# Contracting 192 channels as 128 and 64 instead of 96 and 96, in the second block of a vision tower

## The chip, the cores and the metric

One core of a Trainium2 chip runs the whole kernel. The metric is the device time of one execution in microseconds (us). Before the change it is 1512.79 us, the median of 3 runs (1511.65 to 1516.04).

## The reference, cut to what matters

32 images become 49 tokens of 192 channels each: T = 1568 tokens. The tower has a first block (Mamba, then a soft mixture of 64 experts), which the change doesn't touch, and a second block:

```
h  = LN(x) ;  k = h Wk_a^T ; v = h Wv_a^T ; sr = sigmoid(h Wr_a^T)          (192 -> 192 each)
x  = x + (sr * bi_wkv(decay, first, k, v)) Wo_a^T
h  = LN(x) ;  kf = relu(h Wk_f^T)^2                                         (192 -> 768)
x  = x + sigmoid(h Wr_f^T) * (kf Wv_f^T)                                    (receptance, 768 -> 192)
h  = LN(x) ;  q, k, v = split(h in_w^T + in_b) ; 12 heads of 16, softmax over the 49 tokens of an image
x  = x + ctx out_w^T + out_b
x  = x + MLP(x) ;  x = x + mixture of 4 experts, 192 -> 768 -> 192 each
```

All of it is float32.

## The kernel before, in words

Every engine runs a program written by hand: the order on each engine is the order of the code, and semaphores carry the dependences. A `Stage` is a row of PSUM results: `fill` makes TensorE wait until the bank's last result was taken, `wait_filled` and `wait_taken` are the two sides, and `plan` gives each result its bank (eight of them) and the engine that takes it. A step below is one matrix multiplication of the program; in the profile it has two records, since its operands are float32.

Tokens stand in 16 tiles of 98 (two images), and in 4 quarters of 392 (NT = 16, QT = 392; half `h` is quarters 2h and 2h+1). What is contracted over channels must have channels on partitions, so each LayerNorm's output is turned by TensorE. In the parts that the change touches it is turned as two chunks of 96 channels (`transposed`, `turn`), and ScalarE copies it out of PSUM with LayerNorm's gain and bias (`turned_in` into `xaT`, `turned_x5` into `x5T` and, every image twice, into `x5two`). Each product is then two steps of 96 rows into one PSUM bank. The MLP and the experts at the end of the kernel already contract 128 and 64 rows (`packed`, `hidden_tiles`, `xmA`, `xmB`): four 128-row steps, then four 64-row steps that lie by turns on partitions 0 to 63 and 64 to 127.

The second block in order, by the functions of TensorE's program:

- `turn(s_xaT)`, `kvr_in(0)`, `kvr_in(1)`, `turn(s_xaT)`, then a loop over 6 units of `arguments`, `kvr_in(t + 2)` and `sums`. Units with `j == 0` make 128 of the 192 outputs for one quarter; units 2 and 3 make the last 64 outputs for two quarters, side by side in the array's columns. VectorE scans (`front`, `back`, `final`), ScalarE exponentiates.
- For each half: `turn(s_xbT)`, `receptance` (8 tiles, outputs of 98 x 192), `channel_hidden` (12 outputs of 128 x 392, taken by ScalarE with Relu and squared by VectorE), then `wkv_out(1)` in the first half only, and `channel_out`, which waits for `kf_ready`. `wkv_out` is the one function of this part that contracts 128 and then 64 rows already, by turns.
- `turn(s_x5T)` and `queries_keys` for each half (8 outputs of 96 x 392), with VectorE's `twice_normed` ahead of the turn. ScalarE takes them in `qk_out`; GpSimd spreads the keys into blocks (`kblk`, L907).
- The attention loop, one iteration for each of 16 pairs of images. TensorE: `value_rows(i)`, `score_rows(i)`, `prob_turn(i-1)`, `context_rows(i-2)`, `context_turn(i-3)`, `attention_out(i-4)`. VectorE: `values`, `less_max` (L1759, L1763), `context`, `sums`. ScalarE: `probs(i)` (Exp, L1298), `probs_t(i-1)`, `ctx_t(i-3)`. From iteration 4 on, the bank of `value_rows(i)` is the one that `ctx_t(i-4)` empties, and `ctx_t(i-4)` stands behind `probs(i-1)` on ScalarE.
- The bias of queries, keys and values is a 97th row: `in_w[CH]` holds it and `x5T`, `x5two` have a row of ones, which GpSimd writes (L894, L895).

L1876 is `mm`, L1885 the transposes of `transposed`, L923 ScalarE's `copy_out`, L1275 the doubled copy of `turned_x5`, L1386 `normalise`.

## Time and profile before

| | |
|---|---|
| median of 3 runs | 1512.79 us |
| the profiled execution, its own time | 1509.02 us |
| its span, first to last instruction | 1507.3 us |
| TensorE busy | 1323.9 us, 88% of the span |
| VectorE, ScalarE, GpSimd busy | 915.8, 670.9, 554.6 us |
| the second block up to the MLP | 895 to 1215 us of the span |

The profile is one execution. A busy TensorE says that a record was open, not that the array was full: ends of its records are modelled and overlap the next ones, so the pace is read from how many records start in a stretch. PE is TensorE, PEld its weight loads, DVE VectorE, ACT ScalarE, POOL GpSimd. PEclk is the granted share of TensorE's clock (1.00 is 2.4 GHz).

### The profile page before, as it was taken

What the parts mean: (1) busy time and instruction counts of PE and PEld (TensorE: products, weight loads), DVE (VectorE), ACT (ScalarE), POOL (GpSimd) and SP (SyncE); (2) the same over time, 40 slices, a digit from 0 to 9 for tenths busy, and PEclk for the clock granted to TensorE, in tenths of its full rate; (3) what the DMA queues carried; (4) which work ended last, traced back from release to release, by engine and by line L of the source; (5) the groups of instructions that cost most, each with busy time, mean ns of one, the idle gap of its engine ahead of it and who ended that gap; (6) DMA issues with size and microseconds to landing.
All of it is one profiled execution on the core that took longest, in us unless ns stands there. A gap on an engine that the chain in (4) does not pass through costs nothing.

```text
span 1507.3 us, 18440 instructions
## 1 busy us (share of the span) xinstructions
PE 1323.9 (88%) x6684; PEld 767.2 (51%) x6684; DVE 915.8 (61%) x1513; ACT 670.9 (45%) x1206; POOL 554.6 (37%) x399
## 2 busy tenths in 40 slices
PE   7979989898989867469988859979999999999998
PEld 6634445454545434244433445547856659445444
DVE  3789999999999999972100148855446624221022
ACT  4786767677777744042110117631552241313311
POOL 1478898988989887300000020012034302000000
PEclk9999999999999999769999969999999999999999
DMA  6405051422414040344999940000010001030101
GB/s 205 172 2 172 12 162 37 135 75 98 127 46 171 12 160 0 138 178 189 395 397 396 372 103 0 1 0 1 1 38 1 2 1 31 7 110 13 37 0 33
DMA packets 38773, 151.96 MB, mean 101 GB/s; under 512 B 10364, under 2 KB 14587, under 8 KB 33948
## 3 DMA queue, kind: packets, MB, share of 16 engines
q1 hardware_dynamic: 34588, 149.21, 27.6%
q10 hardware_dynamic: 4096, 1.58, 0.4%
q8 instruction: 54, 0.88, 0.2%
q14 instruction: 35, 0.29, 0.1%
HBM read 147.56 MB, written 1.63 MB: 99 GB/s over the span
## 4 chain that ended last, share of the span: by engine, by line
PE 54%; DVE 20%; issue 10%; ACT 6%; DMA 5%; POOL 4%; SPq 1%; ACTq 0%; DVEq 0%; POOLq 0%
PE ps L1876 52%; DVE arena L1474 7%; DVE arena L1463 5%; DMA arena<-in_e_b 4%; POOL arena L821 3%; ACT arena L923 2%; ACT ps L1034 1%; DVE stats L1371 1%; DVE arena L1759 1%; PE ps L1885 1%; ACT arena L928 1%; DVE arena L1483 1%; SPq L633 1%; DVE arena L1763 0%; DVE arena L1514 0%
## 5 line engine op out<-in xcount | busy, mean ns | idle before, releaser
L1876 PE MATMUL ps<-arena 128*32 128x192 f32 (+17 forms) x5236 | 946.4, 415 | 97.8 <-DVE arena L1524 22.2
L1876 PEld LDWEIGHTS ps<-arena 128*32 128x32 f32 (+15 forms) x5236 | 539.7, 154 | 475.7 <-issue 277.1
L821 POOL TENSOR_TENSOR arena<-arena 128x784 f32<-128x784 f32 x192 | 368.9, 1935 | 94.0 <-DVE arena L1474 93.4
L1876 PE MATMUL ps<-arena,ident 128*128 128x392 f32 x900 | 349.3, 517 | 48.3 <-POOL arena L821 40.0
L1474 DVE TENSOR_TENSOR_SCAN arena<-ps,arena 128x784 f32<-128x784 f32 x192 | 341.0, 1777 | 2.5 <-ACT ps L1034 2.5
L1876 PEld LDWEIGHTS ps<-arena,ident 128*128 128x128 f32 x900 | 169.6, 196 | 196.5 <-POOL arena L821 70.5
L1034 ACT ACTIVATE ps<-arena 128x384 f32<-128x384 f32 x384 | 207.9, 575 | 114.2 <-DVE arena L1474 113.4
L923 ACT ACTIVATE arena<-ps 128x392 f32<-128x392 f32 (+9 forms) x265 | 124.3, 487 | 294.7 <-PE ps L1876 206.2
L923 ACT ACTIVATE arena<-ps,arena 128x392 f32<-128x392 f32 (+2 forms) x191 | 103.4, 602 | 224.5 <-PE ps L1876 139.1
L1463 DVE TENSOR_TENSOR arena<-ps,arena 128x784 f32<-128x784 f32 x192 | 182.8, 953 | 8.0 <-ACT ps L1060 6.8
L1622 DVE COPY arena<-ps 128x384 f32<-128x384 f32 x32 | 16.3, 552 | 150.7 <-PE ps L2124 150.7
L1852 DVE SCALAR_TENSOR_TENSOR arena<-ps,arena 128x392 f32<-128x392 f32 x16 | 10.0, 626 | 127.3 <-PE ps L1876 112.0
L891 POOL TENSOR_TENSOR h<-h,arena 98x384 f32<-98x384 f32 x8 | 8.0, 996 | 152.5 <-DVE arena L1699 152.5
L907 POOL TENSOR_TENSOR arena<-arena 96x294 f32<-96x294 f32 x64 | 41.6, 681 | 56.8 <-PE ps L1876 53.5
L855 POOL MEMSET arena<- 128x128 f32 x1 | 0.2, 205 | 124.8 <-ACT arena L923 124.8
L873 POOL TENSOR_SCALAR arena<-arena 128x4 f32<-128x4 f32 x1 | 0.2, 236 | 122.7 <-DMA arena<-in_first 122.7
L1885 PE MATMUL ps<-ident,arena 98*96 98x98 f32 x160 | 21.9, 283 | 23.5 <-ACT arena L1146 17.3
L1298 ACT ACTIVATE arena<-arena 113x588 f32<-113x588 f32 x16 | 11.1, 694 | 62.5 <-DVE arena L1763 62.5
L1785 DVE TENSOR_TENSOR arena<-arena,ps 98x192 f32<-98x192 f32 x32 | 11.1, 354 | 45.6 <-PE ps L1876 44.0
L914 POOL TENSOR_TENSOR h<-h,arena 98x192 f32<-98x192 f32 x16 | 9.3, 593 | 71.7 <-DVE arena L1785 71.7
L1885 PEld LDWEIGHTS ps<-ident,arena 98*96 98x96 f32 x160 | 17.4, 145 | 30.6 <-ACT arena L1146 18.8
L923 ACT ACT_TABLE_LOAD x10 | 12.8, 1283 | 45.2 <-PE ps L1876 45.1
(201 smaller groups left out, 861.0 us busy)
## 6 DMA issues: line engine op xcount, KB each, us to landing
arena<-in_e_w SPq DMA_DIRECT2D x32, 2304.0 KB
arena<-bc_rows SPq DMA_DIRECT2D x128, 392.0 KB, 4.8
arena<-in_patches SPq DMA_DIRECT2D x4, 1176.0 KB, 7.5
arena<-comb_rows SPq DMA_DIRECT2D x1, 3136.0 KB, 10.7
arena<-in_mlp_w SPq DMA_DIRECT2D x5, 576.0 KB, 4.6
arena<-arena ACTq DMA_DIRECT2D x128, 12.0 KB, 8.6
arena<-in_mlp_w SPq DMA_DIRECT2D x5, 384.0 KB, 3.6
arena<-in_mlp_w SPq DMA_DIRECT2D x10, 192.0 KB, 4.0
```

The source lines that it names most:

```text
L633: sp.dma_start(dst, src).then_inc(loaded[key], 16)
L821: pool.tensor_tensor(pair(hbuf[:, at % SLOTS, :]), pair(hbuf[:, at % SLOTS, :]), c_all[:, n:n + 2, :], ALU.mult).then_inc(times_c, 1)
L907: pool.tensor_tensor(kblk[:, 4 * (i % 2) + 2 * j + c, :].rearrange("p (h l) -> p h l", l=TOKENS), kT[:, c, at:at + TOKENS].unsqueeze(1).br ...
L923: act.activation(dst, src, func, **kw).then_inc(s.taken["act"], 1)
L928: ins = act.activation(dst[r][:, k, :], ident[:, :], ACT.Copy, scale=values(k))
L1034: ins = act.activation(steps_of(two(DECAY[at % 2], 128, HALF)[:, j * QT:(j + 1) * QT])[:, :, lo:lo + TOKENS - 1], steps_of(dt[:, s % 2, c, ...
L1371: own.step(dve.bn_stats(stats[:, t, :], src[:, i, :]))
L1463: TT(pair(hbuf[:, at % SLOTS, :]), bank(DU_BANK, 128, 0, QT).unsqueeze(1).broadcast_to([128, 2, QT]), b_all[:, 2 * p:2 * p + 2, :], ALU.mu ...
L1474: dve.tensor_tensor_scan(hbuf[:, at % SLOTS, :][:, way], dA[:, way], hbuf[:, at % SLOTS, :][:, way], 0.0, ALU.mult, ALU.add).then_inc(scan ...
L1622: dve.tensor_copy(hidT[:, g % 2, 3 * k:3 * k + 3, :].rearrange("p k n -> p (k n)"), bank(s_hT.banks[i][0], 128, 0, 384)).then_inc(s_hT.tak ...
L1876: return pe.matmul(dst, lhsT, rhs, start=first, stop=last)
L1885: ins = pe.transpose(bank(s.banks[i][0], parts, t * TILE, (t + 1) * TILE), src[:, 4 * q + t, chunk(c)], ident[0:TILE, 0:TILE])
```

## The change

Channel mix, receptance, and attention's queries, keys and values contract 128 and 64 rows. The turned activations become a wide tensor (128 rows, all tokens) and a narrow one (channels 128 to 191 of quarters 2h on partitions 0 to 63, of quarters 2h+1 on 64 to 127); each narrow weight stands twice, on both halves of the partitions. `packed` turns each half as wide, wide, narrow, narrow, so a product waits for a later item of the turn. The 97th rows are gone: `qk_out` adds the bias of queries and keys, and `ctx_t`, now two activations instead of one, that of the values. GpSimd's two memsets go, one load less is issued in group `tb`, and the channel-mix products come out by hidden chunk instead of by quarter, so `channel_out` waits for nearly all squares.

```diff
-        xaT = R.take(CH, [2, T])
+        xaA = R.take(128, [T])
+        xaB = R.take(128, [HALF])
...
-                        s_xaT.wait_taken(pe, 2 * q + 1)
-                        for c in range(2):
-                            ins = mm(bank(s_kvr.banks[i][0], 128, 0, QT), w_kvr[:, c, w * D:w * D + 128],
-                                     xaT[:, c, quarter(q)], c == 0, c == 1)
+                        h, k = divmod(q, 2)
+                        s_xaT.wait_taken(pe, 4 * h + 2 + k)
+                        dst, rows = bank(s_kvr.banks[i][0], 128, 0, QT), slice(64 * k, 64 * k + 64)
+                        mm(dst, w_kvr[:, 0, w * D:w * D + 128], xaA[:, quarter(q)], True, False)
+                        ins = mm(dst, w_kvr[rows, 1, w * D:w * D + 128], xaB[rows, h * QT:(h + 1) * QT], False, True)
...
             def receptance(k):
 
+                s_xbT.wait_taken(pe, 4 * k + 3)
+                for first in range(4 * k, 4 * k + 4, 2):
+                    both = [(n, 2 * pair_at(n) + j) for j in range(2) for n in (first, first + 1)]
+                    for n in (first, first + 1):
+                        s_rf.fill(pe, n)
+                    for n, tile in both:
+                        dst = bank(s_rf.banks[n][0], TILE, tile % 2 * D, (tile % 2 + 1) * D)
+                        p0 = 64 * (tile // TQ % 2)
+                        at = tile // 8 * QT + tile % TQ * TILE
+                        mm(dst, xaA[:, cols(tile)], w_rf[:, 0, :], True, False)
+                        ins = mm(dst, xaB[p0:p0 + 64, at:at + TILE], w_rf[p0:p0 + 64, 1, :], False, True)
+                        if tile % 2 == 1:
+                            ins.then_inc(s_rf.filled, 1)
+
+            def channel_hidden(k):
+
+                for first in range(12 * k, 12 * k + 12, 4):
+                    for i in range(first, first + 4):
+                        _, m, j = WIDE[i]
+                        s_kf.fill(pe, i)
+                        mm(bank(s_kf.banks[i][0], 128, 0, QT), w_kf[:, 0, 128 * m:128 * m + 128],
+                           xaA[:, quarter(2 * k + j)], True, False)
+                    for i in range(first, first + 4):
+                        _, m, j = WIDE[i]
+                        rows = slice(64 * j, 64 * j + 64)
+                        mm(bank(s_kf.banks[i][0], 128, 0, QT), w_kf[rows, 1, 128 * m:128 * m + 128],
+                           xaB[rows, k * QT:(k + 1) * QT], False, True).then_inc(s_kf.filled, 1)
...
-                    pe.wait_ge(kf_ready, 6 * (i // 2) + 6)
+                    pe.wait_ge(kf_ready, 12 * k + 11 + i // 2 % 2)
...
             def value_rows(i):
                 s_vb.fill(pe, i)
                 for j in range(2):
-                    at = (2 * i + j) * TILE
-                    for k in range(2):
-                        rows = CH + k
-                        ins = mm(bank(s_vb.banks[i][0], TILE, j * D, (j + 1) * D),
-                                 x5two[0:rows, k, at:at + TILE],
-                                 in_w[0:rows, k, 2 * D:3 * D], k == 0, k == 1)
+                    image = 2 * i + j
+                    p0 = 64 * (image // 8 % 2)
+                    at = (image // 16 * 8 + image % 8) * TILE
+                    dst = bank(s_vb.banks[i][0], TILE, j * D, (j + 1) * D)
+                    mm(dst, x5twoA[:, image * TILE:(image + 1) * TILE], in_w[:, 0, 2 * D:3 * D], True, False)
+                    ins = mm(dst, x5twoB[p0:p0 + 64, at:at + TILE], in_w[p0:p0 + 64, 1, 2 * D:3 * D], False, True)
...
             def ctx_t(i):
                 v = bank(s_cx.banks[i][0], CH, 0, 2 * 128).rearrange("p (c j q) -> p c j q", c=2, j=2)
-                copy_out(s_cx, i, ctxT[0:CH, :, cols(i)].rearrange("p c (j l) -> p c j l", j=2),
-                         v[:, :, :, 0:TOKENS])
+                s_cx.wait_filled(act, i)
+                for c in range(2):
+                    ins = act.activation(ctxT[0:CH, c, cols(i)].rearrange("p (j l) -> p j l", j=2),
+                                         v[:, c, :, 0:TOKENS], ACT.Identity, bias=in_b[:, 4 + c:5 + c])
+                ins.then_inc(s_cx.taken["act"], 1)
```

`kvr_in`'s units 2 and 3 become, for each of k, v and r, two wide steps side by side and then two narrow ones side by side. `queries_keys` is written like `channel_hidden`: four wide steps, then four narrow ones, two groups to a half; `queries_keys` waits for the fourth item of the turn. `turned_x5` still makes two activations for each of its 8 items.

The order on TensorE from the first half's receptance to the first half's `channel_out` (ps2 and ps3 hold the receptance, then `channel_hidden` runs through the banks). Before:

```order
L1885 MATMUL ps0<-ident,arena 96x98 x8
L1885 MATMUL ps1<-ident,arena 96x98 x8
L1876 MATMUL ps2<-arena 98x192 x8
L1876 MATMUL ps3<-arena 98x192 x8
L1876 MATMUL ps0<-arena 128x392 x4
L1876 MATMUL ps1<-arena 128x392 x4
L1876 MATMUL ps2<-arena 128x392 x4
L1876 MATMUL ps3<-arena 128x392 x4
```

And in the changed kernel, at the same place:

```order
L2193 MATMUL ps0<-ident,arena 128x98 x8
L2193 MATMUL ps1<-ident,arena 128x98 x8
L1897 MATMUL ps2<-arena 98x192 x8
L1897 MATMUL ps3<-arena 98x192 x8
L1897 MATMUL ps0<-arena 128x392 x2
L1897 MATMUL ps1<-arena 128x392 x2
L1897 MATMUL ps0<-arena 128x392 x2
L1897 MATMUL ps1<-arena 128x392 x2
```

The number of steps is the same everywhere. In `channel_hidden` four banks are opened by wide steps and then closed by narrow ones; in the receptance the rows read alike, and inside them wide and narrow steps now take turns.

The order on ScalarE in the attention loop, one iteration (Exp, the copy of the turned probabilities, the turned context). Before:

```order
L1298 ACTIVATE arena<-arena 113x588
L923 ACTIVATE arena<-ps3 98x678
L923 ACTIVATE arena<-ps0 96x2x98
```

In the changed kernel:

```order
L1316 ACTIVATE arena<-arena 113x588
L937 ACTIVATE arena<-ps3 98x678
L1330 ACTIVATE arena<-ps0,arena 96x98 x2
```

The turned context is taken by two activations with a bias where one copy stood.

## Rows read from the trace of the kernel before

**Rows 1.** The page: busy time of each engine, and the chain that ended last.
```profile
PE 1323.9 (88%) x6684; PEld 767.2 (51%) x6684; DVE 915.8 (61%) x1513; ACT 670.9 (45%) x1206; POOL 554.6 (37%) x399
PE 54%; DVE 20%; issue 10%; ACT 6%; DMA 5%; POOL 4%; SPq 1%; ACTq 0%; DVEq 0%; POOLq 0%
```

**Rows 2.** The chain that ended last, second block: start us, us, what.
```profile
898.62 9.66 PE ps L1876 x24
...
940.51 54.15 PE ps L1876 x172
...
1009.81 44.78 PE ps L1876 x208
```

**Rows 3.** Windows: stretch, length, PE, PEld, DVE, ACT, POOL busy (xcount), PEclk, DMA.
```profile
1009.82:1015.09 5.27, 5.27 (x32) 5.27 (x33) 0.00 (x0) 2.55 (x5) 0.00 (x0) 1.00 0.02 3
1015.10:1030.89 15.79, 15.79 (x49) 9.09 (x49) 6.24 (x11) 5.96 (x12) 0.00 (x0) 1.00 0.00 0
1030.90:1038.74 7.84, 7.84 (x33) 3.85 (x31) 2.23 (x4) 0.50 (x1) 2.99 (x3) 1.00 0.01 2
1295.34:1301.33 5.99, 5.99 (x16) 0.70 (x16) 1.84 (x3) 0.00 (x0) 0.00 (x0) 1.00 0.00 0
1363.71:1368.04 4.33, 4.33 (x18) 2.11 (x16) 0.00 (x0) 1.94 (x6) 0.00 (x0) 1.00 0.00 0
```

**Rows 4.** Timeline of the turns: start us, us, engine line, [idle before <-releaser].
```profile
895.48 3.14 PE L1885 MATMUL ps<-ident,arena 98*96 98x98 f32 x16 [4.09 <-DVE arena L1386]
896.78 2.55 ACT L923 ACTIVATE arena<-ps,arena 96x392 f32<-96x392 f32 x4 [23.17 <-PE ps L1885]
...
1008.52 2.38 ACT L923 ACTIVATE arena<-ps,arena 96x392 f32<-96x392 f32 x4 [7.98 <-PE ps L1885]
```

**Rows 5.** Timeline of the turn ahead of queries and keys, second half.
```profile
1100.18 0.18 DVE L1361 SCALAR_TENSOR_TENSOR rs<-rs_tmp,rs 98x16 f32<-98x16 f32 x1
1100.34 5.21 POOL L907 TENSOR_TENSOR arena<-arena 96x294 f32<-96x294 f32 x8 [3.25 <-ACT arena L923]
1100.39 0.67 DVE L1359 SCALAR_TENSOR_TENSOR rs_tmp<-var,rs 98x16 f32<-98x16 f32 x1
1103.00 3.82 DVE L1386 TENSOR_SCALAR arena<-h,mv,rs 98x192 f32<-98x192 f32 x8
...
1107.52 1.00 ACT L1275 ACTIVATE arena<-ps,arena 96x784 f32<-96x784 f32 x1
1108.41 0.67 ACT L923 ACTIVATE arena<-ps,arena 96x392 f32<-96x392 f32 x1
```

**Rows 6.** Windows again: second half's queries and keys; the attention loop's 16 starts.
```profile
1109.13:1121.37 12.24, 12.24 (x32) 5.93 (x33) 0.00 (x0) 9.38 (x19) 0.00 (x0) 0.86 0.00 1
1121.38:1207.80 86.42, 79.78 (x757) 55.57 (x755) 55.72 (x120) 23.60 (x45) 36.41 (x56) 1.00 0.01 1
```

**Rows 7.** Timeline of one iteration of the attention loop, and the next one's start.
```profile
1172.04 2.69 PE L1876 MATMUL ps<-arena 96*98 96x192 f32 x16 [0.41 <-ACT arena L923]
1173.52 0.69 PEld L1876 LDWEIGHTS ps<-arena 96*64 96x64 f32 x8 [0.25 <-issue]
...
1175.58 0.83 DVE L1763 TENSOR_TENSOR arena<-ps,arena 113x294 f32<-113x294 f32 x2
1176.45 0.69 ACT L1298 ACTIVATE arena<-arena 113x588 f32<-113x588 f32 x1 [4.46 <-DVE arena L1763]
1177.05 0.93 ACT L923 ACTIVATE arena<-ps 98x678 f32<-98x678 f32 x2
1178.04 2.68 PE L1876 MATMUL ps<-arena 96*98 96x192 f32 x16 [0.41 <-ACT arena L923]
```

**Rows 8.** Groups by line and shape, 880 to 1300 us: xcount, busy us, mean ns.
```profile
L923 ACT ACTIVATE arena<-ps 128x392 f32<-128x392 f32 x64 | 31.7, 497 | 42.2 <-PE ps L1876 40.2 <-PE ps L2393 2.0
L923 ACT ACTIVATE arena<-ps,arena 128x392 f32<-128x392 f32 x58 | 31.1, 594 | 55.6 <-PE ps L2393 30.5 <-PE ps L1876 25.0
...
L923 ACT ACTIVATE arena<-ps 96x196 f32<-96x196 f32 x16 | 5.1, 321 | 3.1 <-PE ps L2359 3.1
```

More of the change, by code:

```diff
@@ L316, in build_tower @@
         mlp2b = R.take(TILE, [D])
-        aff5 = R.take(CH, [2, 2])
+        aff5 = R.take(128, [2, 2])
+        in_b = R.take(CH, [6])
         aff_m = R.take(128, [2, 2])
@@ L1199, in turned_in @@
                 for i in some:
-                    q, c = divmod(i, 2)
-                    copy_out(s, i, xaT[:, c, quarter(q)], bank(s.banks[i][0], CH, 0, QT),
-                             ACT.Identity, bias=aff[:, row + 1, c:c + 1], scale=aff[:, row, c:c + 1])
+                    rows, c = rows_of(i)
+                    copy_out(s, i, turned(i, xaA, xaB), turning(s, i),
+                             ACT.Identity, bias=aff[rows, row + 1, c:c + 1], scale=aff[rows, row, c:c + 1])
             def kvr_out(u):
@@ L2160, in _, with packed @@
                 ins.then_inc(s_mix.filled, 1)
+            def packed(s, src, ready, some=range(8)):
+                flat = src.rearrange("p t n -> p (t n)")
+                for i in some:
+                    h, c, k = i // 4, i // 2 % 2, i % 2
+                    s.fill(pe, i)
+                    for t in range(TQ):
+                        at = 8 * h + TQ * k + t
+                        ready(at + 1 if c == 1 and k == 0 else at)
+                        lo = at * D + (0 if c == 0 else 128 if k == 0 else 64)
+                        ins = pe.transpose(bank(s.banks[i][0], 128, t * TILE, (t + 1) * TILE),
+                                           flat[:, lo:lo + 128], ident[0:TILE, 0:TILE])
+                    ins.then_inc(s.filled, 1)
             def kvr_in(u):
@@ L2261, in turn @@
             def turn(s, src, ready, k):
-                transposed(s, src, lambda i: pe.wait_ge(ready, i + 1), some=range(4 * k, 4 * k + 4))
+                packed(s, src, lambda i: pe.wait_ge(ready, i + 1), range(4 * k, 4 * k + 4))
             pe.wait_ge(loaded["rw"], 16 * RW_LOADS)
@@ L2291, in _ @@
             pe.wait_ge(loaded["tb"], 16 * TB_LOADS)
-            pe.wait_ge(const_ready, MIX_CONST + 2)
+            pe.wait_ge(const_ready, MIX_CONST + 1)
             def queries_keys(some):
-                for i in some:
-                    q, which, c = i // 4, i // 2 % 2, i % 2
-                    s_x5T.wait_taken(pe, 2 * q + 1)
-                    s_qk.fill(pe, i)
-                    for k in range(2):
-                        rows = CH + k
-                        at = which * D + c * CH
-                        ins = mm(bank(s_qk.banks[i][0], CH, 0, QT), in_w[0:rows, k, at:at + CH],
-                                 x5T[0:rows, k, quarter(q)], k == 0, k == 1)
-                    ins.then_inc(s_qk.filled, 1)
+                for first in range(some.start, some.stop, 4):
+                    h = first // 8
+                    s_x5T.wait_taken(pe, 4 * h + 3)
+                    for i in range(first, first + 4):
+                        at, q = i % 8 // 2 * CH, 2 * h + i % 2
+                        s_qk.fill(pe, i)
+                        mm(bank(s_qk.banks[i][0], CH, 0, QT), in_w[:, 0, at:at + CH], x5A[:, quarter(q)], True, False)
+                    for i in range(first, first + 4):
+                        at, rows = i % 8 // 2 * CH, slice(64 * (i % 2), 64 * (i % 2) + 64)
+                        mm(bank(s_qk.banks[i][0], CH, 0, QT), in_w[rows, 1, at:at + CH],
+                           x5B[rows, h * QT:(h + 1) * QT], False, True).then_inc(s_qk.filled, 1)
             queries_keys(range(8))
```

140 lines of the change are left out of this document (63 added, 77 removed).

## The prediction

> **What bounds the kernel now.** First the page: TensorE is busy for 88% of the span and carries 54% of the chain that ended last [rows 1]. An average over stages says little about five functions, so next the chain itself in the second block: it runs on TensorE alone for 9.66 us of `kvr_in`, for 54.15 us in the loop that holds the other units of `kvr_in`, and for 44.78 us from receptance to `channel_out` [rows 2]. There a step saved or lengthened counts in full. Two places are different. Between `channel_out(1)` and the second half's queries, VectorE's LayerNorm and ScalarE's eight copies bound the time [rows 5]. In the attention loop TensorE waits in every iteration, for ScalarE: the idle time ahead of `value_rows` is ended by ACT L923 [rows 7].
>
> **What a change between 128 and 64 rows costs.** The diff keeps the number of steps. It can gain only where narrow steps stand next to each other on opposite halves, and it loses wherever wide and narrow steps meet. Both are in the trace, in functions written that way already. The first 32 records of `receptance(0)`, all of 96 rows, take 5.27 us, so a step of two records takes 0.33 us [rows 3]. `wkv_out(1)` has as many steps of the same shape, but 128 and 64 rows by turns: 7.84 us, 0.98 us for a pair instead of 0.66 [rows 3]. That is 0.33 us for two changes, 0.165 each. With outputs of 392 columns a step takes 15.79 / 24 = 0.658 us [rows 3]. The experts' group of four wide and four narrow ones takes 4.33 us (4.35 with the windows' edges) [rows 3]; four wide and two double narrow ones would be 6 x 0.658 = 3.95, so two changes cost 0.40. The gate's four pairs, with weights of 4 columns only, take 5.99 us, 1.50 a pair against 1.32: 0.18 for two changes [rows 3]. So a change costs 0.09 us with next to no weights to load, and 0.17 to 0.20 with 98 to 128 columns of them.
>
> The Trainium skill speaks to this on its page "TensorEngine Tiling (Array Packing)", in two places. Tiling Modes, Key Properties: changing the tiling mode, not just the tile, drains the array. By that rule this change pays at each border, and the trace agrees. The page's section on theoretical speedup gives up to 2x for contractions of 64 rows or fewer, which speaks for the change; no function of this trace reaches it over wide and narrow steps together (the experts' group gets 5.26 / 4.35 = 1.21 times).
>
> **The change part by part.**
>
> 1. Turn ahead of `kvr_in(0)`. It waited for item 2 of the turn, now for item 3. ScalarE takes the four in 2.55 us from 896.78, so the third is done at about 898.9, and TensorE starts now at 898.4 [rows 4]. +0.6 us.
> 2. `kvr_in`, four units of one quarter: 12 pairs wide, narrow, never two narrow ones together. Each pair has two changes of 128 columns: 12 x 0.39 = +4.6. Bounds: the gate's 0.18 gives 2.2, the experts' 0.40 gives 4.8; I take the latter's side, since the weights have 128 columns.
> 3. `kvr_in`, two units of 64 outputs: side by side in columns before and after, with two narrow steps between wide ones. Changes go from 2 to 7 a unit. Weights of 64 columns lie between 4 and 98, so 0.14 each: +1.4. The trace doesn't show this change of rows under divided columns: 0 to 2.0.
> 4. Turns ahead of receptance, twice. TensorE waited for two of four items, now for all. ScalarE takes four in 2.38 us from 1008.52, to 1010.90, and receptance started at 1009.81 [rows 2, 4]: +1.1 each, +2.3.
> 5. Receptance, twice 8 pairs. The second tile's narrow step is on the other half, but a wide step stands between, so I price it like `wkv_out`, whose shape it has: 7.84 - 5.27 = 2.6 each, **+5.2**.
> 6. `channel_hidden`, twice: 3 groups of 4.35 instead of 15.79: -2.75 each, **-5.5**. ScalarE and VectorE now take four results in a burst, and `channel_out(1)` waits for nearly all squares instead of half; only a turn lies between: +0.2.
> 7. Queries and keys. The first half's 16 steps lie under VectorE's LayerNorm, so what they save there is worth nothing in itself. The turn behind it now has to be copied out whole: 4 x 1.46 us on ScalarE (an L1275 and an L923, 1107.52 to about 1108.97) instead of 2 x 1.46 [rows 5]. But the keys' blocks on GpSimd start later, since the first key item is now in the second group. Today, when GpSimd starts at 1100.34, VectorE's next small step takes 0.67 us where it took 0.18 just before, and eight `normalise` take 3.82 [rows 5]. Without that the tiles are there some 3 us earlier, and ScalarE starts at about 1104.9, behind the first half's copies, instead of 1106.05. It ends at about 1110.7 instead of letting TensorE go at 1109.13: +1.6. Then 4.35 x 2 = 8.7 us instead of 10.5: -1.8. The stretch of 12.24 us has a granted clock of 0.86 after the idle time [rows 6], and TensorE is idle for longer now: +0.3. Together +0.1, between -2 if nothing else is late and +3 if GpSimd collides as before.
> 8. `value_rows`, 16 iterations. Now 1.48 us from 1172.04 to the scores' first weights at 1173.52 [rows 7], already with a change at the end. Afterwards two of `wkv_out`'s pairs, 1.96 to 1.98: **+0.5** each. What hides it? Nothing: the ring is values and scores on TensorE, maximum and subtraction on VectorE to 1176.41, Exp at 1176.45, two copies from 1177.05 to 1177.98, and `value_rows` at 1178.04, since it waits for the bank that `ctx_t` empties [rows 7]. 16 x 0.5 = **+8.0**. VectorE and GpSimd move with the ring.
> 9. `ctx_t` as two activations with a bias. A copy of 392 columns takes 0.497, of 196 columns 0.321 us, so 0.9 ns a column and 0.23 us for 98; a bias adds 0.594 - 0.497 = 0.10 [rows 8]. Two of 0.33 that overlap by 0.10, like their neighbours, are 0.55 instead of 0.32: +0.22, on the ring for `value_rows(4)` to `value_rows(15)`, 12 x 0.22 = +2.6, and 0.4 in the tail. Bounds 0.15 and 0.35 give 1.8 and 4.6.
> 10. At nothing: the two memsets on GpSimd (they ran under `channel_out(0)`; nothing waited), wider loads of weights (VectorE holds TensorE until 895.48, not a load [rows 4]), transposes of 128 instead of 96 columns, and the bias in `qk_out`, 16 times 0.1 us on an engine that is idle between items; were that cover gone, it would be 0.8 us in the second half.
>
> Sum: 0.6 + 4.6 + 1.4 + 2.3 + 5.2 - 5.5 + 0.2 + 0.1 + 8.0 + 3.0 = **+19.9 us**. The profiled execution took 1509.0 us, so it would take 1529. The median of the runs shown is 3.8 us above it; the forecast for the median is 1512.8 + 19.9, about 1533.
>
> **The rivals.**
>
> - *No border costs anything here, and narrow steps on opposite halves overlap even with a wide one between (faster, 0.04).* This is the tiling page's up to 2x, as a mechanism of this kernel: receptance saves 8 of 32 steps, 8 x 0.33 = -2.6, `channel_hidden` saves 12 x 0.658 = -7.9, the queries' section -0.7, `kvr_in` and `value_rows` nothing; against it 0.6 + 2.3 + 3.0 for the later waits and `ctx_t`, with 0.2 for the squares. -5.1: 1507.7. For it speaks only that receptance goes from half to half on purpose. Against it, `wkv_out`'s 7.84 us. It decides if a wide and narrow pair of receptance takes under 0.6 us, not 0.98.
> - *The borders are free, but nothing overlaps across a wide step (same, 0.03).* Then only item 5 is zero instead of -2.6: -2.5, 1510.
> - *The attention loop absorbs its part (slower by less, 0.12).* TensorE has 0.41 us idle ahead of `value_rows` [rows 7]. If the ring is another than I read, items 8 and 9 are hidden: +8.9, 1522. Against it, TensorE restarts 0.05 us after ScalarE's end in every iteration.
> - *The clock falls as well (slower by more, 0.10).* With more waiting in the loop (79.78 us busy of 86.42 now [rows 6]) the granted clock may not stay at 1.00, as it doesn't behind the idle time of [rows 6]. A tenth of the loop at half clock would be some 8 us: 1541.
> - *The forecast (0.71)*: 1533.
>
> **How the numbers follow.** Bounds of the unknown costs: item 2 -2.4, item 3 -1.4 to +0.6, item 7 -2 to +3, item 9 -1 to +2, and 2 to 3 us between medians. Rarely all one way: 1527 to 1539 for the forecast alone. The range reaches down to the loop that absorbs and up to the clock: 1521 to 1542. A measurement of this kernel can tell about 0.3%, 4.5 us, from no change. Slower: 0.71 + 0.12 + 0.10 = 0.93; same 0.03; faster 0.04.
>
> **What would show it.** In the new profile: an iteration of the attention loop of about 6.7 us instead of 6.0, with 1.98 us from the first value step to the scores; receptance of 7.8 us; `channel_hidden` of 13 us a half; `kvr_in`'s pairs at 1.7 us; VectorE's small steps ahead of the last turn at 0.18 us throughout. The forecast is wrong if receptance's 32 records take about 5 us, or if iterations stay at 6.0 us.

## The result, and the profile after

The changed kernel takes 1562.59 us in the median (1555.98 to 1584.12, 4 runs), beside 1513.40 for the kernel before (1511.65 to 1516.04, 4 runs): a ratio of 1.0309, interval 1.0249 to 1.0369. Every ratio here and below leaves out executions over 1.5% above the fastest of their kernel (one of the four here, three of ten for `ctx_t` as two activations alone, two of four for receptance grouped). The profiled execution took 1555.98 us against 1509.02, +47.0. The forecast was 1533 and its range ended at 1542. The four executions of the changed kernel differ by 28 us among themselves, and the longer ones have the lower mean granted clock (0.934 at 1555.98 us, 0.912 at 1584.12). Only the first was profiled; a trace of a later execution of the same kernel, below, differs from it in the attention loop.

First the page: busy time, the granted clock over the 40 slices, and the chain's shares. They answer to [rows 1]. TensorE is busy for 35 us more with the same 6684 records, and its share of the chain is still over half.

```profile
PE 1359.1 (87%) x6684; PEld 761.8 (49%) x6684; DVE 910.7 (59%) x1513; ACT 675.2 (43%) x1222; POOL 548.9 (35%) x397
...
PEclk9989999999999999689999769969999979989999
...
PE 52%; DVE 19%; issue 10%; ACT 7%; POOL 5%; DMA 5%; SPq 1%; ACTq 0%; DVEq 0%; POOLq 0%
```

Next the chain that ended last in the second block (start us, us, what), which answers to [rows 2]. `kvr_in(0)` and `kvr_in(1)` are 19.28 us where they were 9.66, receptance to `channel_out` 50.89 where it was 44.78.

```profile
896.13 19.28 PE ps L1897 x24
...
1026.02 50.89 PE ps L1897 x208
...
1079.85 21.05 PE ps L1897 x80
```

The windows of the changed kernel say what the steps cost at either clock (columns as in [rows 3]). TensorE is idle for 4.09 us ahead of the turn (first line, timeline), as in the kernel before [rows 4]; then the turn and the 24 records of `kvr_in` run at a granted clock of 0.50 (1.2 GHz) from end to end, 3.20 us a pair. Two pairs of `kvr_in` at 1.00 (2.4 GHz) take 3.41 us, a unit of 64 outputs takes 4.84. Receptance of the second half takes 7.80 at 1.00; what stands at the same place in the first half, 36 records, takes 15.39 at 0.56.

```profile
892.26 3.66 PE L2193 MATMUL ps<-ident,arena 98*128 98x98 f32 x16 [4.09 <-DVE arena L1407]
```

```profile
896.13:915.34 19.21, 19.21 (x24) 5.97 (x24) 15.11 (x50) 3.05 (x6) 0.00 (x0) 0.50 0.00 1
...
1026.02:1041.41 15.39, 15.39 (x36) 7.32 (x37) 0.00 (x0) 1.96 (x4) 0.00 (x0) 0.56 0.00 0
1079.80:1087.60 7.80, 7.75 (x32) 3.94 (x32) 5.77 (x32) 1.47 (x3) 0.00 (x0) 1.00 0.01 2
...
956.83:960.24 3.41, 3.41 (x9) 1.18 (x8) 3.38 (x5) 0.99 (x2) 0.00 (x0) 1.00 0.01 2
926.67:931.51 4.84, 4.84 (x25) 1.18 (x24) 4.81 (x9) 1.58 (x3) 0.00 (x0) 1.00 0.00 0
```

One iteration of the attention loop, from the timeline, answers to [rows 7]. From the first value step at 1201.25 to the scores' weights at 1203.23 are 1.98 us, where they were 1.48. `ctx_t` is two activations in 0.56 us, and TensorE's idle time ahead of `value_rows` is 0.65 us, ended by them. From Exp to Exp it is 6.75 us.

```profile
1199.42 0.69 ACT L1316 ACTIVATE arena<-arena 113x588 f32<-113x588 f32 x1 [4.97 <-DVE arena L1784]
...
1200.64 0.56 ACT L1330 ACTIVATE arena<-ps,arena 96x98 f32<-96x98 f32 x2
...
1201.25 3.19 PE L1897 MATMUL ps<-arena 128*98 128x192 f32 x16 [0.65 <-ACT arena L1330]
...
1203.23 0.69 PEld L1897 LDWEIGHTS ps<-arena 96*64 96x64 f32 x8 [0.25 <-issue]
...
1206.17 0.69 ACT L1316 ACTIVATE arena<-arena 113x588 f32<-113x588 f32 x1 [4.97 <-DVE arena L1784]
```

**Where the 47 us lie.** Seven stretches, each between marks that both traces have (the first transpose of a turn, the first and the last Exp; for receptance's first turn the first step of the last `sums`, which stands right ahead of it, 4 us before its first transpose):

| stretch | before, us | after, us | more | forecast |
|---|---|---|---|---|
| start to the second block's first turn | 895.5 | 892.3 | -3.2 | 0 |
| to receptance's first turn (`kvr_in` lies here) | 108.6 | 126.1 | +17.5 | +6.6 |
| to receptance's second turn | 50.3 | 58.4 | +8.1 | +1.0 |
| to the turn ahead of `channel_out(1)` | 22.9 | 24.0 | +1.1 | +1.0 |
| to the first Exp (queries and keys) | 48.5 | 48.3 | -0.2 | +0.3 |
| first to last Exp | 80.7 | 92.6 | +12.0 | +10.1 |
| last Exp to the end | 300.9 | 312.6 | +11.7 | +0.9 |

Where the clock is 1.00 the forecast fits. The rest stands where the granted clock is 0.50. Read in windows of 1 us, it is at 0.50 behind 891 us for 30.7 us (6.8 in the kernel before), at 1014 and 1028 us for 23.9 (6.8, at 1001), at 1130 for 6.8 (3.4, at 1110), from 1236 to 1260 for 23.9 (none), and behind 1320 for 13.6 (3.4). The stretch from 1236 begins in the loop and covers its end:

```profile
1241.69:1260.00 18.31, 18.24 (x127) 15.11 (x124) 5.71 (x16) 6.78 (x16) 0.00 (x0) 0.50 0.00 1
```

### The profile page after: what moved, and what is told of

Same layout as the page of the kernel before. It is cut to its first block, busy times and chain, and to the rows that moved or that the text cites. A ratio compares the mean times of both kernels' runs of the same rounds, so it can differ in the third digit from the quotient of the medians.

```text
span 1554.3 us, 18438 instructions
## 1 busy us (share of the span) xinstructions
PE 1359.1 (87%) x6684; PEld 761.8 (49%) x6684; DVE 910.7 (59%) x1513; ACT 675.2 (43%) x1222; POOL 548.9 (35%) x397
## 4 chain that ended last, share of the span: by engine, by line
PE 52%; DVE 19%; issue 10%; ACT 7%; POOL 5%; DMA 5%; SPq 1%; ACTq 0%; DVEq 0%; POOLq 0%
PE ps L1897 50%; DVE arena L1495 7%; DVE arena L1484 5%; DMA arena<-in_e_b 4%; POOL arena L837 4%; ACT arena L937 2%; PE ps L2193 1%; ACT ps L1048 1%; DVE arena L1535 1%; DVE arena L1780 1%; ACT arena L942 1%; DVE stats L1392 1%; DVE arena L1504 1%; SPq L650 1%; POOL arena L848 0%
## 5 line engine op out<-in xcount | busy, mean ns | idle before, releaser
L1897 PE MATMUL ps<-arena 128*32 128x192 f32 (+17 forms) x5236 | 974.8, 421 | 107.4 <-ACT arena L937 24.4
L1897 PEld LDWEIGHTS ps<-arena 128*32 128x32 f32 (+16 forms) x5236 | 528.9, 156 | 522.9 <-issue 330.9
L937 ACT ACTIVATE arena<-ps 128x392 f32<-128x392 f32 (+9 forms) x233 | 111.1, 498 | 298.7 <-PE ps L1897 199.3
L937 ACT ACTIVATE arena<-ps,arena 128x392 f32<-128x392 f32 (+2 forms) x207 | 112.2, 601 | 246.5 <-PE ps L1897 159.9
L1806 DVE TENSOR_TENSOR arena<-arena,ps 98x192 f32<-98x192 f32 x32 | 11.1, 354 | 49.6 <-PE ps L1897 48.3
L1768 DVE TENSOR_TENSOR arena<-ps,arena 98x384 f32<-98x384 f32 x16 | 8.9, 558 | 47.1 <-PE ps L1897 47.1
L1731 DVE TENSOR_TENSOR arena<-arena 128x392 f32<-128x392 f32 x24 | 12.0, 562 | 36.5 <-ACT arena L937 36.5
```

Source lines behind the costliest of these rows:

```text
L937: act.activation(dst, src, func, **kw).then_inc(s.taken["act"], 1)
L1897: return pe.matmul(dst, lhsT, rhs, start=first, stop=last)
```

## The experiments

Two theories on why the clock is low for so long. A border is a place where a 128-row step and a 64-row step meet. **A:** places thick with borders between 128-row and 64-row steps hold it down. **B:** TensorE waits longer (for whole turns, for `ctx_t`), and that lets it fall. In all figures below the ratio is to the kernel before on the same chip.

**The changed kernel again.**

> The changed kernel as it is, once more, to see how far its executions differ. From 890 us on the profile of the changed kernel had a granted clock of half speed for 99 us, where the kernel before had it for 20 us. Theory A (the borders between 128-row and 64-row steps hold the clock down, wherever they are dense): 1555 to 1570 us, half clock again in kvr_in and receptance. Theory B (the longer waits of TensorE let the clock fall, and where it falls is a matter of phase): the same mean, but the stretches at half clock move about between executions.

1574.26 us (1571.18 to 1578.39, 4 runs), 1.0389 [1.0357, 1.0421]. The stretches up to the loop repeat within 2 us (125.1 for 126.1, 59.9 for 58.4). The loop doesn't: it runs at 0.50 from 1197 us to its end and beyond, 85.3 us in one go. Windows of the loop:

```profile
1150.53:1196.90 46.37, 42.25 (x374) 25.03 (x372) 28.11 (x60) 13.95 (x29) 21.80 (x34) 1.00 0.00 1
1196.95:1264.07 67.12, 67.12 (x342) 39.89 (x343) 24.79 (x52) 11.30 (x24) 12.97 (x20) 0.50 0.00 1
```

An iteration is 6.74 us at 1.00 and 10.23 at 0.50: 3.5 us lost in each. The median is over the 1570 expected at most: the loss in the loop varies more than one trace told.

**The waits alone.** The kernel before, waiting for later items of the turns:

```diff
-                        s_xaT.wait_taken(pe, 2 * q + 1)
+                        s_xaT.wait_taken(pe, 3 if q < 2 else 7)
-                    s_xbT.wait_taken(pe, 2 * (i // 2) + 1)
+                    s_xbT.wait_taken(pe, 4 * k + 3)
-                    s_x5T.wait_taken(pe, 2 * q + 1)
+                    s_x5T.wait_taken(pe, 4 * (q // 2) + 3)
```

> The kernel before, without any border more, but with the changed kernel's waits on the turns: kvr_in, receptance and queries_keys wait for the last item of their half instead of the second. Structure alone: 0.6 + 2.3 + 3 = 6 us more. Theory A: the clock stays as it was, 1518 to 1521 us, half speed for 20 to 30 us from 890 us on. Theory B: the clock falls as in the changed kernel, 1535 us or more with 60 us or more at half speed.

1519.71 us (1517.09 to 1526.22, 10 runs), 1.0037 [1.0019, 1.0056]. The stretch of `kvr_in` is 111.4 us, 2.8 more than before, and at 0.50 for 10.2 us behind 895. Theory A's number. The waits at the turns cost what they are long and take the clock down by little: from 890 to 1300 us its trace is at 0.50 for 30.6 us, that of the kernel before for 17.0, that of the changed kernel for 85.2.

**`value_rows` without borders.** The changed kernel, its narrow step on all 128 rows, with zero weights in the other half:

```diff
-                    ins = mm(dst, x5twoB[p0:p0 + 64, at:at + TILE], in_w[p0:p0 + 64, 1, 2 * D:3 * D], False, True)
+                    ins = mm(dst, x5twoB[:, at:at + TILE], in_w2 if p0 else in_w[:, 1, 2 * D:3 * D], False, True)
```

> The changed kernel with one thing other: value_rows contracts its 64 channels over all 128 rows, with weights that are zero on the other half's 64 rows, so it has no border between 128-row and 64-row steps and the same number of steps. The ring's own price goes back by 0.5 us an iteration (6.74 to about 6.24 us), 8 us in all. Theory A (borders hold the clock down): no stretch at half clock in the attention loop in any profile, so a median of 1540 to 1548 us beside some 1574 for the changed kernel. Theory B (longer waits do it; the loop's second activation for ctx_t stays): the 8 us alone, 1562 to 1567 us, half clock still in the loop.

1546.06 us (1543.99 to 1550.96, 4 runs), 1.0233 [1.0204, 1.0262]. An iteration is 6.23 us instead of 6.74: the borders of `value_rows` cost 0.51 us, forecast 0.5. The time is what theory A gave. TensorE still waits 0.65 us ahead of `value_rows`, and yet the clock is 1.00 all over the loop in the trace; that it was so in all four executions is taken from their narrow spread. The edit takes away the borders and puts more rows to work at once, so it doesn't tell these two apart:

```profile
1156.41:1239.65 83.24, 74.27 (x728) 51.84 (x724) 52.35 (x113) 24.62 (x53) 34.86 (x54) 1.00 0.01 1
```

**`ctx_t` as two activations, alone.** The kernel before with that part (bias zero):

```diff
-                copy_out(s_cx, i, ctxT[0:CH, :, cols(i)].rearrange("p c (j l) -> p c j l", j=2),
-                         v[:, :, :, 0:TOKENS])
+                s_cx.wait_filled(act, i)
+                for c in range(2):
+                    ins = act.activation(ctxT[0:CH, c, cols(i)].rearrange("p (j l) -> p j l", j=2),
+                                         v[:, c, :, 0:TOKENS], ACT.Identity, bias=act_c[0:CH, 5:6])
+                ins.then_inc(s_cx.taken["act"], 1)
```

> The kernel before, with ctx_t as two activations with a bias (of zeros), as in the changed kernel, and nothing else. An iteration of the attention loop goes from 6.00 to 6.24 us, so 3 to 4 us more in both theories. Theory A: 1517 to 1518 us and no half clock in the loop. Theory B: the longer wait of TensorE brings half clock into the loop, 1525 us or more.

An iteration of 6.24 us, +0.24 (forecast +0.22), and 1512.8 us of span in the profiled execution. But the ten executions go from 1508.21 to 1546.61, median 1524.14, where thirteen of the kernel before stay within 1507.58 to 1520.05. The ratio is 1.0038 [1.0003, 1.0074]. The three longest (1539 to 1547 us) have a mean granted clock of 0.926 to 0.932, the others 0.944 to 0.958. The profiled one is among the short ones, at 1.00 all over the loop, so where the clock was lost in the long ones isn't shown. No step of TensorE was changed, so theory A alone doesn't fit the loop.

**Receptance grouped by height.** The changed kernel, each two tiles' steps as wide, narrow, narrow, wide:

```diff
-                        mm(dst, xaA[:, cols(tile)], w_rf[:, 0, :], True, False)
-                        ins = mm(dst, xaB[p0:p0 + 64, at:at + TILE], w_rf[p0:p0 + 64, 1, :], False, True)
+                    order = [(0, both[0:2]), (1, both[0:2]), (1, both[2:4]), (0, both[2:4])]
...
+                                ins = mm(dst, xaA[:, cols(tile)], w_rf[:, 0, :], step < 2, step >= 2)
...
+                                ins = mm(dst, xaB[p0:p0 + 64, at:at + TILE], w_rf[p0:p0 + 64, 1, :],
+                                         step >= 2, step < 2)
```

> The changed kernel with receptance in groups: two wide steps, four narrow ones that lie by turns on either half, two wide ones, so 2 borders for 4 tiles in place of 8. A half's receptance goes from 7.84 to about 4.6 us at full clock, 6.5 us less in both theories. Theory A: the half clock behind the turn of the first half (1026 to 1043 us) is shorter as well, another 3 to 5 us there. Theory B: it stays for 14 to 17 us.

1566.01 us (1533.56 to 1580.27, 4 runs), 1.0212 [1.0128, 1.0296]: the total says little, since the executions differ by 47 us. The profiled execution has a loop at 1.00 and a span of 1531.8. Its two stretches of receptance are 48.80 and 20.69 us instead of 58.39 and 24.03, both under the kernel before (50.3, 22.9). In the second half, at 1.00 on either side, that is 3.3 us (3.25 expected). In the first it is 9.6, so some 6 us come from the clock, more than theory A's 3 to 5; the half clock at 1028 us is gone:

```profile
1016.70:1065.50 48.80, 47.65 (x230) 33.79 (x231) 19.64 (x60) 9.31 (x20) 3.98 (x4) 0.94 0.00 1
1065.51:1086.20 20.69, 19.11 (x98) 11.27 (x95) 12.57 (x48) 8.08 (x18) 0.00 (x0) 1.00 0.00 1
```

**`kvr_in` on 128 rows throughout** (the other half's weights zero, so no borders; it also waits for the last item of the turn):

```diff
-                        ins = mm(dst, w_kvr[rows, 1, w * D:w * D + 128], xaB[rows, h * QT:(h + 1) * QT], False, True)
+                        ins = mm(dst, low[:, w * D:w * D + 128], xaB[:, h * QT:(h + 1) * QT], False, True)
```

> The changed kernel with kvr_in's 64 channels contracted over all 128 rows with zeros in the weights: no border in kvr_in. Own price of its borders: 6 us less (24 changes of 0.2 and 14 of 0.14). Theory A: the stretch at half clock from 893 to 921 us shrinks to the 7 to 10 us that the kernels without borders have, another 9 us: 15 us less in all. Theory B: 6 us less, the stretch stays as long in time as TensorE has waited ahead of it.

1559.76 us (1556.72 to 1567.35, 4 runs), 1.0327 [1.029, 1.0363]. The stretch of `kvr_in` falls from 126.1 to 110.9 us, the half clock behind 891 us from 30.7 to 10.2. The total hardly moves, because the loop was at 0.50 for 65 us in the profiled execution.

**`kvr_in` grouped.** Is it the borders, or the 64-row steps? The same steps and rows as the change, in another order, and into three PSUM banks instead of two by turns:

```diff
-                        mm(dst, w_kvr[:, 0, w * D:w * D + 128], xaA[:, quarter(q)], True, False)
-                        ins = mm(dst, w_kvr[rows, 1, w * D:w * D + 128], xaB[rows, h * QT:(h + 1) * QT], False, True)
+                for w in range(3):
...
+                        mm(bank(s_kvr.banks[i][0], 128, 0, QT), w_kvr[:, 0, w * D:w * D + 128],
+                           xaA[:, quarter(q)], True, False)
...
+                for w in range(3):
...
+                        ins = mm(bank(s_kvr.banks[i][0], 128, 0, QT), w_kvr[rows, 1, w * D:w * D + 128],
+                                 xaB[rows, h * QT:(h + 1) * QT], False, True)
```

> The changed kernel, with each unit of kvr_in written as three wide steps and then three narrow ones, into three banks: 2 changes of height a unit instead of 6, the same steps and rows. From the first turn of the second block to the first turn ahead of receptance the changed kernel takes 126.1 us, the one before 108.6, and the changed one with 128 rows in every step of kvr_in 110.9. If borders are what costs and what holds the granted clock down (theory A), this stretch falls to 112 to 117 us and the half clock behind 891 us lasts 10 us instead of 31. If it is the 64-row steps themselves, fewer rows at work, that hold the clock down, only 16 borders of 0.2 go, and the stretch is 121 to 124 us. The whole time scatters with the attention loop, 1540 to 1575.

1558.30 us (1556.44 to 1562.59, 4 runs), 1.0302 [1.0279, 1.0325]. The stretch is 110.45 us; 6.8 us of it at 0.50 behind 892. `kvr_in(0)` and `kvr_in(1)` take 9.63 us instead of 19.28. It is the borders: the rows at work are the same, and the third bank isn't it, since the run on 128 rows kept two banks and took 110.9. 15.6 us come back, where the borders saved are worth some 5 us at 1.00 (four units with 4 changes less each and two with 5 less, 26 of 0.2 us or less). The second window is the loop, again at half clock:

```profile
893.75:1004.20 110.45, 102.17 (x346) 54.67 (x347) 91.27 (x202) 64.42 (x109) 3.98 (x4) 0.96 0.00 1
...
1196.30:1261.10 64.80, 64.73 (x357) 42.54 (x357) 22.78 (x52) 14.14 (x32) 7.80 (x12) 0.50 0.00 1
```

All sixteen traces of this case agree on `kvr_in` and the first receptance. `kvr_in` by turns (five traces) is at 0.50 for 27.3 to 30.7 us; grouped (five), for 6.8; without borders (six), for 6.8 to 10.2. Every trace has 6.8 to 10.2 us at 0.50 around the turn ahead of the first receptance; in the receptance behind it, steps by turns (six traces) have another 13.6 to 17.1, steps grouped or on 96 rows (ten) none or 3.4.

`value_rows` with its own steps grouped (two wide, then two narrow) was planned, alone and with the other two groupings, and has no measured time. So in the loop the borders were only ever taken away by padding to 128 rows.

**A longer ring without a border.** The kernel before, with `ctx_t` as four activations:

```diff
+                for c in range(2):
+                    for j in range(2):
+                        at = i * TILE + j * TOKENS
+                        ins = act.activation(ctxT[0:CH, c, at:at + TOKENS], v[:, c, j, 0:TOKENS],
+                                             ACT.Identity, bias=act_c[0:CH, 5:6])
```

> The kernel before, with ctx_t cut into four activations instead of one copy: the attention loop's ring is made longer on ScalarE alone, no step of TensorE is changed, and the output is the same. Two activations made an iteration 6.24 us instead of 6.00; four should make it about 6.6 to 6.7, as long as the changed kernel's 6.74. If longer waits of TensorE in the loop are what lets the granted clock fall there (theory B for the loop), some iterations take some 10 us at half clock in most executions, the executions scatter, and the median lies between 1530 and 1565. If borders between 128-row and 64-row steps are what does it (theory A for the loop), the granted clock stays at 1.00 over the loop, and the time is 1514 + 12 x 0.65 + 1, about 1523, with little scatter.

1544.55 us (1535.67 to 1546.67, 4 runs), 1.0188 [1.0157, 1.0219]: theory B's range, for the loop of this kernel. An iteration is 6.53 us, a little less than the 6.6 expected. TensorE is idle for 0.94 us ahead of `value_rows` (timeline), 0.41 before. The granted clock is 1.00 for the first nine iterations, and from 1173.7 us it is 0.50 (windows), with 9.49 us an iteration. The other three executions weren't traced; their times and mean granted clocks (0.927 to 0.935, beside 0.947 to 0.955 for the kernel before) say the same of them:

```profile
1166.23 0.85 ACT L1315 ACTIVATE arena<-ps,act_c 96x49 f32<-96x49 f32 x4
...
1167.13 2.68 PE L1882 MATMUL ps<-arena 96*98 96x192 f32 x16 [0.94 <-ACT arena L1315]
```

```profile
1124.20:1173.70 49.50, 42.77 (x421) 29.82 (x417) 31.74 (x68) 17.79 (x47) 24.43 (x38) 1.00 0.01 1
1173.74:1227.87 54.13, 54.13 (x293) 37.62 (x295) 21.04 (x44) 10.89 (x30) 10.38 (x16) 0.50 0.00 1
```

**Neither in the loop.** The changed kernel with `value_rows` on 128 rows, as above, and `ctx_t` as one copy, as in the kernel before.

> The changed kernel, with value_rows contracting 128 rows twice (the second time half of them zero weights, so no border) and ctx_t as one copy again; the bias of the values is left out of the computation. An iteration should be 6.00 us, as before the change. Theory B for the loop: no wait is longer than before, so the loop's granted clock is 1.00 in every execution, and the time is that of the kernel with value_rows at 128 rows, 1546, less 12 x 0.24 and 0.4: about 1543, all executions within 8 us. Theory A says the same of the loop, since no border is left in it; both leave the clock's loss in kvr_in and in receptance where it is. If the time is under 1530, the loss in those two stages hung on the loop's state after all, and both are wrong.

1543.04 us (1538.96 to 1549.03, 4 runs), 1.0197 [1.0168, 1.0225], where 1543 was expected. An iteration is 5.99 us at 1.00. `kvr_in` and the first receptance lose as in the changed kernel. That the median hits 1543 is partly luck: the executions differ by 10 us, and in the traced one (1546.94) the second receptance is at 0.50 for 17.1 us too, where no other trace has over 3.4.

**Borders in the loop, no longer wait.** The changed kernel with `kvr_in` and receptance grouped and `ctx_t` as one copy, `value_rows` as in the change. Against it, **the longer wait on 128 rows**: grouped, `value_rows` on 128 rows, `ctx_t` as four activations.

> The changed kernel with kvr_in and receptance grouped by height and ctx_t as one copy (the values' bias is left out of the computation), value_rows with its borders as in the change. An iteration is 6.00 + 0.50 = 6.50 us, as long as in the run with four activations and no border, but made longer by borders in the array and not by a wait. If a longer ring alone lets the clock fall, the two go alike: 1530 to 1550 for both, or 1516 for both. If borders count by themselves, only this one falls; if the drained array counts as work, only the other one does. With the clock at 1.00 over the loop it is 1511.1 + 16 x 0.5 = about 1519.

> The run with three edits (value_rows on 128 rows, no border, an iteration of 6.23 us, 1511.3, twelve executions without a fall in the loop) with ctx_t cut into four activations, as in the run that lengthened the ring of the kernel before: an iteration of about 6.53 us. There, with value_rows on 96 rows, the clock fell in the loop in all four executions (1536 to 1547). If the length of TensorE's wait decides, it falls here too: some iterations of 9.5 us, a median of 1530 to 1550. If it is what the steps have in height (rows 96 against 128), it does not, and the time is 1511.3 + 12 x 0.3 + 1 = about 1516, within 8 us of it.

The first: 1518.23 us (1517.06 to 1522.94, 10 runs), 1.0033 [1.0017, 1.0049]. Iterations of 6.50 us, made longer by borders, TensorE's idle time 0.41 us as before the change: the clock stays at 1.00 over the loop (first row). The second: 1522.26 us (1516.92 to 1526.62, 10 runs), 1.0058 [1.0037, 1.008]. Iterations of 6.53 us, idle time 0.94: two short falls in the loop, 3.4 us each, mean 0.96 (second row). Its time lies between what the two readings gave. With the same 0.94 us the 96-row kernel lost the clock for 72 us in one go.

```profile
1122.03:1210.23 88.20, 81.90 (x730) 48.72 (x728) 52.42 (x113) 21.75 (x41) 34.79 (x54) 1.00 0.01 1
```

```profile
1125.93:1215.65 89.72, 77.51 (x728) 53.93 (x724) 52.33 (x113) 28.18 (x77) 34.80 (x54) 0.96 0.01 1
```

All traces, by TensorE's idle time ahead of `value_rows` and by its steps; time at 0.50 that begins in the loop:

| steps of `value_rows` | 0.41 us | 0.65 us | 0.94 us |
|---|---|---|---|
| 96 rows | none (3 traces) | none (1; three of ten executions long) | 71.7 us (1) |
| 128 rows, padded | none (2) | none (2) | twice 3.4 us (1) |
| 128 and 64 by turns | none (1) | none (1), 23.9 to 85.3 us (4) | not run |

Neither theory stands alone. The borders of `value_rows` without a longer wait lose nothing, and a wait of 0.65 us without them lost nothing on 128 rows; the changed kernel has both, and taking away either one (the padding, or the single copy) takes the fall away. A wait of 0.94 us brings falls with no border, short or long by the steps.

**The account closed.** All four edits: `kvr_in` grouped, receptance grouped, `value_rows` on 128 rows, `ctx_t` as one copy; then the same with the change's two activations and bias, so that nothing is left out.

> The changed kernel with four edits at once: kvr_in's steps grouped by height, receptance's steps grouped by height, value_rows on 128 rows twice, ctx_t as one copy (the bias of the values is left out of the computation). It closes the account. The kernel with the last two took 1543.0; grouping kvr_in took 15.6 us off its stretch (126.1 to 110.5), grouping receptance 9.6 and 3.4 off the two stretches of the receptance (58.4 to 48.8, 24.1 to 20.7). If the lost time is made of these pieces alone, each in its own place, the sum is 1543.0 - 28.6 = 1514.4, between 1509 and 1519, with the half clock behind 891 us and behind 1010 us as short as in the kernel before, and an iteration of 6.00 us. If taking the clock's loss away in one place only moves it to another, as grouping kvr_in alone seemed to do with the attention loop, it is above 1525.

> As the run with four edits, but with ctx_t as two activations with the values' bias, as in the changed kernel, so that nothing is left out. An iteration is 6.24 us. With the clock at 1.00 over the loop it would be 1514.4 + 3.3 = about 1518. The kernel before with the same two activations had the loop's clock fall in some of its ten executions (1508 to 1547). If the lengthened ring alone brings that, this one scatters as well, 1515 to 1550, with a median of 1518 to 1535; if not, all executions are within 8 us of 1518. Either way it stays above the kernel before with the channel mix alone changed, 1510.5.

1511.11 us (1509.45 to 1515.70, 10 runs), 0.999 [0.9974, 1.0006], and 1511.30 us (1509.75 to 1519.15, 12 runs), 0.9995 [0.9977, 1.0012]. The loss is made up of these pieces, each in its own place (1514.4 expected, 1509 to 1519). The second, at 6.23 us an iteration and 0.65 us of idle time, shows no fall in the loop in its trace and no execution over 1519.15; its median is 7 us under the 1518 expected.

**What of the change pays.** The kernel before, with the channel mix's second part alone: its turn as 128 and 64 rows, receptance grouped, `channel_hidden` in fours. `kvr_in`, queries and keys, `value_rows` and `ctx_t` stay.

```diff
-            turn(s_xbT, xa, xb_ready, 0)
+            turn_xb(0)
             receptance(0)
             channel_hidden(0)
```

> The kernel before, with the part of the change that should pay alone: the second turn of each half as 128 and 64 rows, receptance with steps in groups of like height (wide, narrow, narrow, wide; two tiles' narrow ones on opposite halves), channel_hidden in fours as in the changed kernel. kvr_in, queries_keys, value_rows and ctx_t stay as they were. With receptance so grouped the changed kernel took 69.5 us from the turn ahead of receptance to the turn ahead of the second half's end, where the kernel before takes 73.2; so this one should be 3.5 us under it: ratio 0.9977, 1510 to 1512. If the longer waits ahead of receptance let the clock fall instead (theory B for that stage), the ratio is 1.000 to 1.003.

1510.48 us (1506.99 to 1516.37, 12 runs), beside 1514.63 (16 runs): 0.9975 [0.996, 0.9989]. It has the lowest ratio of all, and the only interval under 1, but the gain is 0.25%. In its trace the two stretches of receptance and `channel_hidden` take 48.70 and 22.39 us, 71.1 beside 73.2: 2.1 of the 4.2 us. Where the rest comes from isn't shown.

## Why the prediction was wrong

The direction was right, and so was the sum where the clock is at 1.00, nearly term by term. What failed is what the forecast put outside the sum: it priced every border at full clock.

- *A border.* 0.33 to 0.40 us for two. Two pairs of `kvr_in` take 3.41 us at 1.00, 1.71 a pair (forecast 1.7); the same 26 records around a unit of 64 outputs take 5.67 instead of 4.92 us (below): +0.75, for two units 1.5 (forecast 1.4). Receptance 7.80 (7.84). Items 2, 3 and 5 stand at 1.00. (In item 2, 12 x 0.39 is 4.7, not 4.6; nothing hangs on it.)

```profile
927.00 4.92 PE L1876 MATMUL ps<-arena 128*128 128x392 f32 x26
...
925.92 5.67 PE L1897 MATMUL ps<-arena 128*128 128x392 f32 x26
```

- *Waits at the turns.* From the first transpose of the turn to `kvr_in(0)` it is 3.9 us instead of 2.9, +0.9 (item 1: +0.6); to the second receptance 3.1 instead of 1.8, +1.3 (item 4: +1.1). The run with the waits alone, which has one more of them (ahead of queries and keys), took 5.5 us more in the median where 6 were expected.
- *`channel_hidden`.* The second half's stretch is +1.1 us as summed, 7.80 us of receptance and 21.05 for it and the hidden part together, so 13.25 (item 6: 3 x 4.35 = 13.05).
- *Queries and keys.* -0.2 us for +0.3. GpSimd's blocks no longer meet VectorE's small steps, which take 0.17 us throughout (timeline of the changed kernel, in place of the 0.67 us of [rows 5]).

```profile
1124.57 0.17 DVE L1382 SCALAR_TENSOR_TENSOR rs<-rs_tmp,rs 98x16 f32<-98x16 f32 x1
...
1127.77 5.15 POOL L921 TENSOR_TENSOR arena<-arena 96x294 f32<-96x294 f32 x8 [6.84 <-ACT arena L937]
```

- *The loop.* 6.74 us an iteration at 1.00 (forecast "about 6.7"): 0.51 by borders, 0.24 by `ctx_t`. The rival in which the loop absorbs its part is out.
- *The step that failed: "The clock falls as well".* It was a rival with a chance of 0.10 and 8 us, for the attention loop alone ("A tenth of the loop at half clock"), and the forecast's own sum had 0.3 us for the clock, in item 7. Items 2 and 5 price the borders of `kvr_in` and of the first receptance at 1.00, though both come soon behind idle time of TensorE (4.09 us before `kvr_in`'s turn, 7.27 us shortly before receptance's). Measured in the same execution: `kvr_in`'s stretch lost 17.5 - 6.6 = 10.9 us to it, the first receptance's 8.1 - 1.0 = 7.1, the loop 12.0 - 10.1 = 1.9 and what follows 11.7 - 0.9 = 10.8, together 30.7, less 3.2 by which the block began earlier: 27 of the 47 us. The runs confirm two of these places: grouped, with the same steps, `kvr_in`'s stretch is back by 15.6 us and the first receptance's by 9.6, about three times what the borders saved cost at 1.00. (Of the 10.8 some 2.6 or more are probably no effect of the change: behind the last Exp the trace of before has 300.9 us, the nine later ones whose loop stays at 1.00 have 303.5 to 309.6, and behind 1300 us the trace of before is at 0.50 for 3.4 us, every other one for 10.2 or more.)
- Why it was missed: 0.86 in [rows 6] was read as what follows idle time. [Rows 3] had pairs of heights at 1.00 and only 7.84 us long, and nothing in the trace of before has such pairs behind idle time. The price of a border was right; that it also keeps the clock down once it is down stood in no row. And the loop's wait was known (0.41 us), but that 0.65 us together with the borders would be too much was not to be read from a kernel that has neither.
- The Trainium skill, page "TensorE: Matmul & The Clock Gate", Terms: a hardware monitor watches how busy TensorE is and gates its clock. By the rows it is not the busy time of a profile that decides: 19.21 of 19.21 us are busy in `kvr_in` at 0.50, and the same steps grouped leave that level early.
- The rivals on the other side fell with `wkv_out`'s price: a pair of receptance takes 0.98 us.

What stays open: why the fall in the loop is long in one execution and absent in the next of the same kernel, why it takes borders and wait together in the changed kernel, and what the height of the value steps has to do with it. At 0.65 us of idle time three of ten executions of the 96-row kernel were long, at a low mean granted clock, and none of sixteen of the two padded kernels.

## What to carry to other kernels

Count the changes of contraction height, not the steps: put wide ones together and narrow ones together, and open several PSUM banks for it if need be. Behind idle time it matters most: the same stretch took 126.1 us with `kvr_in` by turns and 110.5 with it grouped. In a ring in which TensorE waits for a small copy, the length of that wait can have a second price, the granted clock; a bias moved from a spare row of the product onto that copy was not free here. And split a change that has five places: `channel_hidden` paid, receptance only once it was grouped, the rest did not.

## What the runs showed of the hardware that was not expected

- With TensorE's wait 0.53 us longer in each iteration of a loop that otherwise stays the same (0.94 instead of 0.41 us), the granted clock falls to 0.50 for 71.7 us in the trace, and all four executions are 21 us or more over the median of the kernel before. With 0.24 us more, three of ten are 25 us or more over it, with a low mean clock; their traces weren't taken.
- `kvr_in` by turns, entered at 0.50 after idle time, stays there, with TensorE busy throughout: 27.3 to 30.7 us in five traces; grouped, the same steps leave it after 6.8 in five.
- Borders inside the loop don't do it alone: 6.50 us an iteration with the borders of `value_rows` and 0.41 us of idle time, clock 1.00, ten executions within 6 us. With 0.65 us of idle time the clock falls in four of five traces, and there an iteration takes 10.23 us instead of 6.74.
